# Audio tower: f32 bias rows written by ScalarE, a later read of gamma and beta, and new work lists

## The chip, the cores and the metric

The kernel runs on one core of a Trainium2 chip. The metric is the time of one launch on the device in microseconds. Times are medians of several runs; the profile is one execution of its own.

## What is computed

Sixteen batches of x, 64 channels by 250 steps, go through a depthwise convolution with three taps, a linear map to 128 features and a layer norm; then one attention layer over the 250 tokens of a batch, and a feed-forward layer with lower triangular weights.

```python
def tok(x):                                   # x: (16, 64, 250)
    x_sp = conv3(x, conv_w) + conv_b[None, :, None]          # per channel
    m = einsum('btc,dc->btd', swap(x_sp), lin_w) + lin_b + emb.mean(axis=0)
    return layernorm(m) * ln_g + ln_b                        # over d, 128 wide
def attn(x, kernel):
    WQ, WK, WV = x @ kernel[0], x @ kernel[1], x @ kernel[2]
    QK = einsum('bso,bto->bst', WQ, WK)
    c0 = argmin(sum(QK, axis=2)[0])                          # a row of batch 0
    A = softmax(QK / 8); A[:, c0, :] = 0
    return A @ WV
def ffn(x, W1, b1, W2, b2):
    return gelu(x @ tril(W1).T + b1) @ tril(W2).T + b2
h = tok(x)
h = h + attn(layernorm(h), kernel)
out = h + ffn(layernorm(h), W1, b1, W2, b2)
```

## The kernel before

Two batches are a pair: their 2 x 64 channels fill the 128 partitions, so x is read in eight pairs (k = 0 to 7), and the linear map of both is one product with a block matrix, lin_blk. The 250 tokens of a batch stand on 125 partitions as two tiles (a = 0, 1). All products are f32, but for the bias products below. Everything stays on the chip between input and output.

Each engine has a list of calls at the end of its block, written out by hand (or by a planner) in the order in which it issues; an engine works through its list strictly in order, and semaphores make it wait. So the order of the lists is the schedule.

The steps of a pair k: first_tap (L696, ScalarE; for pairs 0 and 1 own_tap, DVE), second_tap (L988) and third_tap on DVE give the convolution xc. project_bias (L345, TensorE) starts the PSUM bank of the pair with the bias row, the same on all 125 partitions, and project_half (L362) adds the two products of a with start=False. For pair 1 the bias product is f32, mean_w by the centred rows emb_c; for the others it is bf16: DVE splits the row into three bf16 rows (split_hi to row_low, L937 to L961, called from L1095), whose sum with a matrix of ones gives it back. project_first does pair 0 by halves. squares (L687, ScalarE) sums the squares of each token; POOL makes the inverse root (head_root_x, and from pair 3 on shared_root for two norms together); scale_x (DVE) multiplies by root and gamma, and head_beta (DVE, pairs 0 and 1) or add_beta (POOL) adds beta.

The steps of a batch b in attention: moments_1 and gather_1 (DVE), root (POOL), normalize_1 (ScalarE), turn_n1 (TensorE, a transpose), out_n1t (ScalarE), queries and values (TensorE), out_pv (ScalarE; out_p0 and out_v0 for batch 0), scores (TensorE), row_max (DVE), exps (ScalarE), turn_a (TensorE), out_at (ScalarE), attend (TensorE), residual (DVE). Batch 0 also gives the row to be left out: row_sums (TensorE), then find_best and find_place on DVE, on which turn_a(0) waits.

The feed-forward layer goes by turns of a pair (four tiles): moments_2, gather_2 (DVE), second_root (POOL), normalize_2 (DVE), turn_n2 (TensorE), out_n2t (ScalarE), up (TensorE), gelu (ScalarE), down (TensorE), finish (DVE). add_b2 (POOL) has added b2 to the residual before. The last pair has one turn of four tiles, whose down and finish (L1072) are done in two parts of two tiles (down_last, L509).

PSUM has eight banks, all in use: bank_x0 and bank_x1 are shared by taps and projections of the pairs in turn (x_bank, L46), bank_o serves pair 3 and then all attend products, bank_s0 and bank_s1 the scores and later the results y.

SyncE issues the reads of x, the weights and nearly all writes of the output; ScalarE's queue issues the read of tok_w and, second, of rows_sb (gamma, beta and b2, each copied to 125 partitions).

Of the kernel before, what the change touches and what calls it, by code (L numbers as in the profile page):

```python
# [5 lines left out]
ALU = mybir.AluOpType  # L6
# [10 lines left out]
def audio_tower(nc, x, tok_pack, weights, rows, out):  # L17
# [12 lines left out]
    with ExitStack() as ctx:  # L30
# [19 lines left out]
        def x_tile(k, n):  # L50

            b, a = n // 2, n % 2
            if k == 0:
# [15 lines left out]
        y_ps = [t[0:H, :].rearrange("p (n d) -> p n d", d=D) for t in bank_s]  # L69
        y_last = [bank_s[1][0:H, 0:2 * D].rearrange("p (n d) -> p n d", d=D),  # L70
                  bank_at[0:H, 0:2 * D].rearrange("p (n d) -> p n d", d=D)]
# [11 lines left out]
        mean_w = sb("mean_w", [128, H])  # L83
        cb_rest = sb("cb_rest", [C + 1, D])
        cb_hi = sb("cb_hi", [C + 1, D], BF16)
        cb_mid = sb("cb_mid", [C + 1, D], BF16)
        cb_rows = sb("cb_rows", [C + 1, D], BF16)
        ones_b = sb("ones_b", [C + 1, H], BF16)
# [10 lines left out]
        rows_sb = sb("rows_sb", [H, 3 * D])  # L99
        gamma = rows_sb[:, 0:D]  # L100
        beta_4, b2_4 = (rows_sb[:, n * D:(n + 1) * D].unsqueeze(1).broadcast_to((H, 4, D)) for n in (1, 2))
# [60 lines left out]

        def p_sb(b):
            return pv_sb[b % 4][:, 0:T]

        def v_sb(b, a):
# [10 lines left out]
        tri_ready, warm_ready, mean_w_ready, ones_ready, rows_zeroed, means_ready, emb_centred, lin_ready = (  # L177
            sem(n) for n in ("tri_ready", "warm_ready", "mean_w_ready", "ones_ready", "rows_zeroed", "means_ready",
                             "emb_centred", "lin_ready"))
        cb_mm, cb_hi_ready, cb_rest_ready, cb_mid_ready, cb_ready, qk_mm, qk_step, qk_ready, wv_mm, wv_ready, w1_mm, w1_ready = (  # L180
            sem(n) for n in ("cb_mm", "cb_hi_ready", "cb_rest_ready", "cb_mid_ready", "cb_ready", "qk_mm", "qk_step", "qk_ready",
# [23 lines left out]
        def _(sp):  # L205
# [14 lines left out]
            for b in (0, 1):  # L220
                sp.wait_ge(y_ready, NP + b)
                sp.dma_start(out_pairs[NP - 1][0:WIDE, b], hb_rows[0:WIDE, NP - 1, b]).then_inc(out_done, 16)
            sp.wait_ge(out_done, 16 * (2 * NP + 1))

        @block.gpsimd
        def _(pool):
# [33 lines left out]
            def second_root(turn, first, count):  # L260

                cols = slice(4 * first, 4 * (first + count))
                pool.wait_ge(stats2, 2 * (first + count))
                pool.tensor_tensor(ve_2[:, cols], mv_2[:, cols, 1], eps[:, 0:4 * count], ALU.add).then_inc(ve2_ready, 1)
                pool.wait_ge(ve2_ready, turn)
                pool.tensor_tensor(root_2[:, cols], ve_2[:, cols], neg_half[:, 0:4 * count], ALU.pow)\  # L266
                    .then_inc(root2_ready, 1)
# [6 lines left out]
            def add_b2(k):  # L274
                pool.wait_ge(resid_ready, 2 * k + 2)
                pool.tensor_tensor(hb_all[:, k, :, :], h_tiles[:, k, :, :], b2_4, ALU.add).then_inc(hb_ready, 1)  # L276
# [38 lines left out]
            shared_root(2)  # L315
            mask(0)
            mask(1)
            add_b2(0)
            add_beta(5)
            shared_root(3)  # L320
            add_b2(1)
            add_beta(6)
            shared_root(4)
            add_beta(7)
            shared_root(5)
            second_root(1, 0, 2)
            add_b2(2)
            second_root(2, 2, 2)
            add_b2(3)
            add_b2(4)  # L330
            add_b2(5)
            second_root(3, 4, 2)
            second_root(4, 6, 1)
            second_root(5, 7, 1)
            add_b2(6)
            add_b2(7)
        @block.tensor
        def _(pe):
            def keep_warm(count):

                for _ in range(count):
                    nc.tensor.matmul(bank_pv[:, :], warm_l[:, :], warm_r[:, :].unsqueeze(1).broadcast_to((128, 8, 64)),
                                     start=True, stop=True)

            def project_bias(k):  # L345

                dst = x_bank(k)[0:H, :].rearrange("p (a d) -> p a d", d=D)
                before = (0, 0, 1, 0, 4, 6, 10, 12)[k]
                if before:
                    pe.wait_ge(x_scaled, before)  # L350
                if k == 1:
                    nc.tensor.matmul(dst, mean_w[:, :], emb_c[:, :].unsqueeze(1).broadcast_to((128, 4, D)),
                                     start=True, stop=True)
                else:
                    pe.wait_ge(ones_ready, 1)
                    pe.wait_ge(cb_ready, 3)
                    if k >= 4:
# [920 lines left out]
```

## Time and profile before

| | us |
|---|---|
| median of three runs | 94.83 |
| the three runs | 94.83, 94.59, 95.0 |
| the profiled execution | 94.69 |
| its span, first to last instruction | 92.9 |

The granted clock of TensorE is 1.0 in the whole span, the higher of its two levels, 2.4 GHz. The span is what the engines' records cover; the time of an execution is that and 1.8 us around it. DVE is VectorE, ACT ScalarE, POOL GpSimd, SP SyncE; PEld is TensorE's weight load, which runs beside its products. L12 is line 12 of the kernel. Ends of products are modelled, so a busy TensorE is not one at its peak.

### The profile page before, as it was taken

The numbers are of one execution on the slowest core, as the hardware profiler recorded it, in microseconds if no ns is written. First come the engines' busy times: TensorE is split into PE (matmuls) and PEld (weight loads), VectorE is DVE, ScalarE is ACT, GpSimd is POOL, SyncE is SP. The second block draws the span as 40 slices with busy tenths as digits, with TensorE's granted clock in tenths as the row PEclk, the third lists the DMA queues.
The fourth block names the chain that finished last, engine by engine and source line by source line (L and its number), as shares of the span: only waits on it lengthen the run. The fifth ranks groups of instructions, "written<-read, shape, count | busy, mean of one in ns | idle before, by whom it ended". The sixth has DMA issues, their size and how long they took to land.

```text
span 92.9 us, 2013 instructions
## 1 busy us (share of the span) xinstructions
PE 87.2 (94%) x567; PEld 73.9 (80%) x567; DVE 74.4 (80%) x296; ACT 69.3 (75%) x215; POOL 47.8 (51%) x70
## 2 busy tenths in 40 slices
PE   4999699999999999999999999999999999999940
PEld 1356567789999999999999999999997877787840
DVE  3279997999698998869998895988989688793560
ACT  1666799899999969977889976697758983565200
POOL 7006398676554386539525519703996305791000
PEclk9999999999999999999999999999999999999999
DMA  2896000000000000000000000000000003036565
GB/s 17 213 280 212 0 0 4 4 0 0 7 0 0 0 0 0 7 4 0 0 4 4 0 7 0 0 0 0 0 0 7 0 0 110 0 110 169 162 175 167
DMA packets 3973, 3.86 MB, mean 42 GB/s; under 512 B 429, under 2 KB 3962, under 8 KB 3962
## 3 DMA queue, kind: packets, MB, share of 16 engines
q1 hardware_dynamic: 3610, 3.35, 12.8%
q10 hardware_dynamic: 352, 0.38, 1.5%
q8 instruction: 5, 0.08, 0.4%
q14 instruction: 6, 0.05, 0.2%
HBM read 1.68 MB, written 2.05 MB: 40 GB/s over the span
## 4 chain that ended last, share of the span: by engine, by line
PE 80%; DVE 9%; DMA 5%; issue 1%; SPq 0%; DVEq 0%
PE bank_o L483 15%; PE bank_s L458 15%; PE bank_at L470 8%; PE bank_pv L434 7%; PE bank_pv L443 7%; PE bank_s L518 7%; DMA x_all<-x_dram 5%; PE bank_x L366 4%; PE bank_x L496 4%; PE bank_nt L507 4%; PE bank_pv L507 4%; PE bank_nt L423 4%; DVE hb_all L1078 2%; DVE tap_a L994 1%; DVE xc L1000 1%; PE bank_o L366 1%
## 5 line engine op out<-in xcount | busy, mean ns | idle before, releaser
L483 PE MATMUL bank_o<-pv,at_sb 125*125 125x129 f32 x128 | 16.8, 273 | 0.0
L458 PE MATMUL bank_s<-n1t,pv 128*125 128x250 f32 x64 | 16.1, 374 | 0.0
L483 PEld LDWEIGHTS bank_o<-pv,at_sb 125*125 125x125 f32 x128 | 15.6, 187 | 0.1
L772 ACT ACTIVATE a<-bank_s,neg_max 125x250 f32<-125x250 f32 x32 | 13.4, 482 | 1.0 <-DVE neg_max L1039 1.0
L1039 DVE TENSOR_REDUCE neg_max<-bank_s 125x2 f32<-125x500 f32 x16 | 10.7, 668 | 2.2 <-PE bank_s L458 2.1
L458 PEld LDWEIGHTS bank_s<-n1t,pv 128*125 128x125 f32 x64 | 11.0, 187 | 0.9
L780 ACT ACTIVATE at_sb<-bank_at 125x500 f32<-125x500 f32 x16 | 9.6, 597 | 2.4 <-PE bank_at L470 1.8
L276 POOL TENSOR_TENSOR hb_all<-h_all,rows_sb 125x512 f32<-125x512 f32 x8 | 10.9, 1384 | 0.0
L765 ACT ACTIVATE pv<-bank_pv 128x508 f32<-128x508 f32 x15 | 9.0, 602 | 2.1 <-PE bank_pv L443 2.0
L272 POOL TENSOR_TENSOR h_all<-h_all,rows_sb 125x512 f32<-125x512 f32 x6 | 7.6, 1271 | 5.7 <-DVE h_all L1013 5.7
L1050 DVE SCALAR_TENSOR_TENSOR h_all<-bank_o,rinv_keep,h_all 125x128 f32<-125x128 f32 x32 | 9.8, 346 | 0.6
L470 PE MATMUL bank_at<-ident,a 125*125 125x125 f32 x64 | 9.6, 273 | 0.0
L434 PE MATMUL bank_pv<-n1t,qk_w 128*128 128x250 f32 x32 | 9.5, 378 | 0.0
L257 POOL TENSOR_TENSOR root_all<-ve_all,neg_half 125x8 f32<-125x8 f32 (+1 forms) x6 | 9.2, 1541 | 0.5
L518 PEld LDWEIGHTS bank_s<-w_sb,g_sb 128*125 128x125 f32 x60 | 7.4, 187 | 2.1 <-issue 2.1
L443 PE MATMUL bank_pv<-wv_c,n1t 128*125 128x128 f32 x60 | 9.0, 272 | 0.0
L443 PEld LDWEIGHTS bank_pv<-wv_c,n1t 128*125 128x125 f32 x60 | 8.5, 187 | 0.5
L747 ACT ACTIVATE n<-h_all,root_all 125x128 f32<-125x128 f32 x24 | 8.3, 409 | 0.7 <-POOL root_all L257 0.7
L470 PEld LDWEIGHTS bank_at<-ident,a 125*125 125x125 f32 x64 | 8.5, 188 | 0.1
L1068 DVE TENSOR_TENSOR n<-h_all,root 125x512 f32<-125x512 f32 x8 | 7.2, 896 | 1.3 <-POOL root L266 1.3
L692 ACT ACTIVATE squared<-bank_x 125x128 f32<-125x128 f32 x26 | 7.2, 294 | 1.3 <-PE bank_x L412 0.8
L518 PE MATMUL bank_s<-w_sb,g_sb 128*125 128x128 f32 x60 | 7.8, 274 | 0.1
(137 smaller groups left out, 183.7 us busy)
## 6 DMA issues: line engine op xcount, KB each, us to landing
out_dram<-hb_all SPq DMA_DIRECT2D x7, 224.0 KB
x_all<-x_dram SPq DMA_DIRECT2D x8, 125.0 KB, 4.9
out_dram<-hb_all SPq DMA_DIRECT2D x2, 112.0 KB
w_sb<-weights_dram SPq DMA_DIRECT2D x1, 192.0 KB, 5.6
rows_sb<-rows_dram ACTq DMA_DIRECT2D x1, 187.5 KB
out_dram<-hb_all SPq DMA_DIRECT2D x6, 26.0 KB
tok_w<-tok_dram ACTq DMA_DIRECT2D x1, 130.0 KB, 3.1
w_sb<-weights_dram SPq DMA_DIRECT2D x1, 128.5 KB, 5.2
```

The lines of the kernel that those rows point to most:

```text
L257: pool.tensor_tensor(root_all[:, i, lo:8], ve_all[:, i, lo:8], neg_half[:, lo:8], ALU.pow)\
L276: pool.tensor_tensor(hb_all[:, k, :, :], h_tiles[:, k, :, :], b2_4, ALU.add).then_inc(hb_ready, 1)
L434: last = nc.tensor.matmul(p_ps, qk_w[:, :], n1t[b % 2][:, :], start=True, stop=True)
L443: last = nc.tensor.matmul(dst[:, a, 0:D], n1t[b % 2][:, a * H:(a + 1) * H], wv_c[:, :], start=True, stop=True)
L458: last = nc.tensor.matmul(s_ps[b % 2][:, a, :], p_sb(b)[:, a * H:(a + 1) * H], n1t[b % 2][:, :], start=True, stop=True)
L470: last = nc.tensor.transpose(at_ps[:, c, a * H:(a + 1) * H], a_sb[b % 2][:, a, c * H:(c + 1) * H], ident[0:H, 0:H])
L483: last = nc.tensor.matmul(o_ps[:, a, 0:DV], at_sb[:, c, a * H:(a + 1) * H], v_sb(b, c), start=(c == 0), stop=(c == 1))
L518: last = nc.tensor.matmul(dst[:, n, :], g_sb[:, j, col:col + H], w2_t, start=True, stop=True)
L772: last = nc.scalar.activation(a_sb[b % 2][:, a, :], s_ps[b % 2][:, a, :], ACT.Exp, bias=neg_max[b % 2][:, a:a + 1])
L780: nc.scalar.activation(at_sb[:, :, :], at_ps, ACT.Copy).then_inc(at_ready, 1)
L1039: nc.vector.tensor_reduce(neg_max[b % 2][:, :], s_ps[b % 2], AX_X, ALU.max, negate=True)\
L1050: last = nc.vector.scalar_tensor_tensor(h_all[:, b, a, :], o_ps[:, a, 0:D], rinv_keep[:, a:a + 1], h_all[:, b, a, :], ALU.mult, ALU.add)
```

## The change

- ScalarE copies the bias row, an f32 sum over the same product as before but on all 125 partitions, once to SBUF (out_cb) and then writes it four times side by side into the bank of pairs 1 and 3 to 7 (write_bias). project_half waits for that and adds to it. Only pair 2 keeps a bias product, now f32. The bf16 split on DVE, its six instructions and two fills, is gone.
- The first tap of pair 1 moves from DVE to ScalarE; ScalarE does the taps of pairs 1 and 2 ahead of squares(0).
- gamma and beta are read by SyncE behind x of pair 3, b2 alone behind pair 7; ScalarE's queue only reads tok_w.
- The last pair goes through the feed-forward layer in two turns of one batch each (turn gives pair, first tile, count and the batches needed; there are nine turns). The very last results are added tile by tile, into banks at and o, and written by five transfers instead of three.
- The warming products write three banks in turn.
- All four lists are in a new order. In the first half first_tap(4) stands ahead of out_p0, turn_a(0) ahead of the products of pair 5, and squares and normalize_1 come later beside exps; the beginnings of two lists are in the diff.

```diff
-        mean_w = sb("mean_w", [128, H])
+        mean_w = sb("mean_w", [128, 128])
+        cb_sb = sb("cb_sb", [H, D])
...
+        def turn(j):
+            return (j, 0, 4, 2 * j + 2) if j < NP - 1 else (NP - 1, 2 * (j - NP + 1), 2, j + NP)
...
         @block.sync
-            for k in range(2, 5):
+            for k in range(2, 4):
                 sp.dma_start(x_all[:, k, 1:T + 1], x_pairs[k]).then_inc(landed_x[k], 16)
+            sp.dma_start(rows_sb[:, :], rows[:, 0:2 * D].broadcast_to((H, 2 * D))).then_inc(landed_rows, 16)
+            sp.dma_start(x_all[:, 4, 1:T + 1], x_pairs[4]).then_inc(landed_x[4], 16)
             sp.dma_start(w_sb[:, 3 * D:5 * D + 1], weights[:, 3 * D:5 * D + 1]).then_inc(landed_f, 16)
             for k in range(5, NP):
                 sp.dma_start(x_all[:, k, 1:T + 1], x_pairs[k]).then_inc(landed_x[k], 16)
+            sp.dma_start(b2_sb[:, :], rows[:, 2 * D:3 * D].broadcast_to((H, D))).then_inc(landed_b2, 16)
...
         @block.tensor
             def project_bias(k):
-                dst = x_bank(k)[0:H, :].rearrange("p (a d) -> p a d", d=D)
-                before = (0, 0, 1, 0, 4, 6, 10, 12)[k]
...
-                    nc.tensor.matmul(dst, ones_b[:, :], cb_rows[:, :].unsqueeze(1).broadcast_to((C + 1, 4, D)),
-                                     start=True, stop=True)
+                pe.wait_ge(x_scaled, 1)
+                nc.tensor.matmul(x_bank(k)[0:H, :].rearrange("p (a d) -> p a d", d=D), mean_w[:, 0:H],
+                                 emb_c[:, :].unsqueeze(1).broadcast_to((128, 4, D)), start=True, stop=True)
             def project_half(k, a):
                 pe.wait_ge(conv_ready, k + 1)
+                if k != 2:
+                    pe.wait_ge(bias_ready, max(k - 1, 1))
...
             project_first(0)
             bias_row()
+            qk_product()
             project_first(1)
-            project_bias(1)
-            qk_product()
             project_half(1, 0)
             wv_centre()
-            project_bias(2)
             project_half(1, 1)
             qk_centre(0)
-            qk_centre(1)
+            project_bias(2)
             project_half(2, 0)
             project_half(2, 1)
+            qk_centre(1)
             turn_n1(0)
-            project_bias(3)
             project_half(3, 0)
+            queries(0)
             project_half(3, 1)
-            queries(0)
...
         @block.scalar
-            act.dma_start(rows_sb[:, :], rows.broadcast_to((H, 3 * D))).then_inc(landed_rows, 16)
...
+            def out_cb():
+                act.wait_ge(cb_mm, 1)
+                nc.scalar.activation(cb_sb[:, :], bank_s[0][0:H, 0:D], ACT.Copy).then_inc(cb_out, 1)
+            def write_bias(k):
+                act.wait_ge(cb_out, 1)
+                if k >= 4:
+                    act.wait_ge(conv_ready, k + 1)
+                nc.scalar.activation(x_bank(k)[0:H, :].rearrange("p (a d) -> p a d", d=D),
+                                     cb_sb[:, :].unsqueeze(1).broadcast_to((H, 4, D)), ACT.Copy).then_inc(bias_ready, 1)
...
+            first_tap(1)
+            first_tap(2)
             squares(0)
+            out_cb()
+            write_bias(1)
+            write_bias(3)
             squares(1)
-            first_tap(2)
+            out_wv()
             out_qk(0)
-            first_tap(3)
             squares(2)
             out_qk(1)
+            first_tap(3)
             squares(3)
+            normalize_1(0)
             out_qk(2)
-            normalize_1(0)
-            out_wv()
             squares(4)
+            out_n1t(0)
             squares(5)
-            out_n1t(0)
+            spread_rows()
             normalize_1(1)
-            spread_rows()
+            first_tap(4)
             out_p0()
...
         @block.vector
             own_tap(0)
             second_tap(0)
             third_tap(0)
-            own_tap(1)
             second_tap(1)
+            second_tap(2)
             third_tap(1)
-            split_hi()
-            split_rest()
-            split_mid()
-            row_hi()
-            row_low()
+            third_tap(2)
             scale_x(0)
-            row_mid()
             head_beta(0)
-            second_tap(2)
             moments_1(0)
             gather_1(0)
             scale_x(1)
-            third_tap(2)
             head_beta(1)
...
-            finish(7, 0)
-            finish(7, 1)
+            finish(7)
+            finish(8)
+            finish(9)
```

## Rows read from the trace of the kernel before

**Rows 1.** The page: busy time and share of each engine.
```profile
PE 87.2 (94%) x567; PEld 73.9 (80%) x567; DVE 74.4 (80%) x296; ACT 69.3 (75%) x215; POOL 47.8 (51%) x70
```

**Rows 2.** Windows: stretch, length, busy us of each engine, clock, DMA share, GB/s.
```profile
18.00:24.00 6.00, 5.94 (x35) 5.30 (x34) 5.57 (x24) 6.00 (x23) 4.07 (x6) 1.00 0.01 3
24.00:30.00 6.00, 6.00 (x47) 5.68 (x47) 5.06 (x23) 5.97 (x23) 3.23 (x4) 1.00 0.00 0
30.00:36.00 6.00, 6.00 (x47) 5.65 (x46) 5.67 (x24) 5.25 (x15) 4.09 (x6) 1.00 0.00 0
36.00:44.00 8.00, 8.00 (x53) 7.38 (x52) 6.62 (x27) 6.92 (x25) 4.62 (x5) 1.00 0.01 3
```

**Rows 3.** Chain of waits: start, length in us, what; from 13.50 to 88.26 TensorE.
```profile
13.50 1.14 PE bank_o L366 x4
...
15.92 0.84 PE bank_s L458 x4
...
22.70 0.44 PE bank_at L470 x4
...
86.50 1.76 PE bank_s L518 x16
...
89.53 0.42 DVE hb_all L1078
```

**Rows 4.** The same chain: bias products of pairs 4 and 6.
```profile
18.21 0.40 PE bank_x L359
...
34.14 0.22 PE bank_x L359
```

**Rows 5.** Timeline of the head: start, length, engine, line, what.
```profile
6.41 0.28 ACT L692 ACTIVATE squared<-bank_x 125x128 f32<-125x128 f32 x1 [0.80 <-PE bank_x L412]
...
7.15 0.28 DVE L940 CAST cb_hi<-bank_s 65x128 bf16<-65x128 f32 x1
...
7.51 0.71 POOL L235 TENSOR_TENSOR root_head<-ve_head,neg_half 125x2 f32<-125x2 f32 x1
...
8.45 0.61 DVE L1013 SCALAR_TENSOR_TENSOR h_all<-bank_x,root_head,rows_sb 125x128 f32<-125x128 f32 x2
...
12.05 0.68 ACT L747 ACTIVATE n<-h_all,root_head 125x128 f32<-125x128 f32 x2
```

**Rows 6.** Timeline of ScalarE behind it: two of four squares, out_p0, the tap.
```profile
12.90 0.28 ACT L692 ACTIVATE squared<-bank_x 125x128 f32<-125x128 f32 x1
...
13.42 0.28 ACT L692 ACTIVATE squared<-bank_x 125x128 f32<-125x128 f32 x1
...
15.19 0.37 ACT L726 ACTIVATE pv<-bank_pv 128x250 f32<-128x250 f32 x1
...
15.46 0.56 ACT L703 ACTIVATE bank_x<-x_all,tok_w 128x250 f32<-128x250 f32 x1
...
15.95 0.26 ACT L692 ACTIVATE squared<-bank_o 125x128 f32<-125x128 f32 x1
```

**Rows 7.** Windows of the loads; landing of x of pairs 2 to 4.
```profile
4.00:4.50 0.50, 0.50 (x2) 0.15 (x1) 0.47 (x2) 0.50 (x4) 0.00 (x0) 1.00 0.56 98
...
6.50:7.00 0.50, 0.50 (x4) 0.26 (x2) 0.47 (x2) 0.49 (x4) 0.00 (x0) 1.00 1.09 370
...
DMA to landing us min/median/max: 5.3/5.4/5.5
```

**Rows 8.** Groups: the copy into at_sb (busy, mean ns); timeline: find_place.
```profile
L780 ACT ACTIVATE at_sb<-bank_at 125x500 f32<-125x500 f32 x16 | 9.6, 597 | 2.4 <-PE bank_at L470 1.8
...
21.61 0.42 DVE L971 FIND_INDEX8 best_at<-best,bank_at 125x8 uint32<-125x250 f32 x1
```

**Rows 9.** Timeline of the end; what SyncE waits for last (us, times, longest).
```profile
81.15 1.75 DVE L1068 TENSOR_TENSOR n<-h_all,root 125x512 f32<-125x512 f32 x1 [0.58 <-POOL root L266]
...
88.82 0.60 PE L518 MATMUL bank_at<-w_sb,g_sb 128*125 128x128 f32 x4
...
SPq L30 <- DMA out_dram<-hb_all: 2.1, 1, 2.1
```

More of the change, by code:

```diff
@@ L272, in add_beta, with add_b2 @@
                 pool.tensor_tensor(h_tiles[:, k, :, :], h_tiles[:, k, :, :], beta_4, ALU.add).then_inc(h_ready, 1)
-            def add_b2(k):
-                pool.wait_ge(resid_ready, 2 * k + 2)
-                pool.tensor_tensor(hb_all[:, k, :, :], h_tiles[:, k, :, :], b2_4, ALU.add).then_inc(hb_ready, 1)
+            def add_b2(j):
+                k, first, count, batches = turn(j)
+                tiles = slice(first, first + count)
+                pool.wait_ge(landed_b2, 16)
+                pool.wait_ge(resid_ready, batches)
+                pool.tensor_tensor(hb_all[:, k, tiles, :], h_tiles[:, k, tiles, :], b2_4[:, 0:count, :], ALU.add).then_inc(hb_ready, 1)
             def mask(n):
@@ L494, in turn_n2 @@
                     pe.wait_ge(n2t_ready, j - 1)
-                for n in range(4):
-                    last = nc.tensor.transpose(t2_ps[j % 2][:, n * H:(n + 1) * H], n2[:, j, n, :], ident[0:H, 0:H])
+                k, first, count, _ = turn(j)
+                for n in range(count):
+                    last = nc.tensor.transpose(t2_ps[j % 2][:, n * H:(n + 1) * H], n2[:, k, first + n, :], ident[0:H, 0:H])
                 last.then_inc(t2_mm, 1)
@@ L579, in _ @@
             scores(4)
+            queries(5)
+            project_half(5, 1)
+            values(5)
+            turn_a(3)
             turn_n1(6)
-            queries(5)
-            values(5)
             attend(2)
-            turn_a(3)
+            scores(5)
             queries(6)
-            scores(5)
-            project_bias(6)
             values(6)
@@ L827, in _ @@
+            out_n1t(2)
+            exps(0)
             first_tap(5)
-            out_n1t(2)
+            normalize_1(3)
+            out_pv(2)
+            out_at(0)
+            out_n1t(3)
+            exps(1)
+            normalize_1(4)
+            out_pv(3)
+            normalize_1(5)
+            write_bias(5)
+            out_n1t(4)
             squares(8)
-            normalize_1(3)
-            exps(0)
-            out_pv(2)
             squares(9)
-            out_n1t(3)
-            normalize_1(4)
@@ L850, in _ @@
             first_tap(6)
-            out_n1t(6)
-            out_pv(5)
-            normalize_1(7)
+            out_at(3)
             exps(4)
-            out_at(3)
+            out_pv(6)
+            out_n1t(7)
+            write_bias(6)
             normalize_1(8)
-            out_n1t(7)
-            out_pv(6)
+            first_tap(7)
+            exps(5)
+            out_pv(7)
+            out_at(4)
             normalize_1(9)
-            exps(5)
-            out_at(4)
-            first_tap(7)
+            out_n1t(8)
@@ L1150, in _ @@
             moments_1(8)
-            second_tap(6)
             moments_1(9)
+            moments_2(1)
             gather_1(8)
             gather_1(9)
+            residual(2)
+            second_tap(6)
+            row_max(5)
             third_tap(6)
-            moments_2(0)
-            residual(2)
-            row_max(5)
             scale_x(10)
-            moments_2(1)
+            scale_x(11)
             residual(3)
-            scale_x(11)
+            moments_2(2)
+            second_tap(7)
+            moments_2(3)
+            moments_1(10)
+            third_tap(7)
             row_max(6)
-            second_tap(7)
-            third_tap(7)
-            moments_1(10)
             moments_1(11)
@@ L1202, in _ @@
             residual(9)
[L1203 removed]
             moments_2(8)
[L1205 to L1210 removed]
+            moments_2(9)
             gather_2(6)
             gather_2(7)
[L1213 removed]
+            row_max(12)
+            normalize_2(1)
+            residual(10)
+            row_max(13)
+            normalize_2(2)
+            residual(11)
+            row_max(14)
```

440 lines of the change are left out of this document (201 added, 239 removed).

## Prediction

> **What bounds the kernel now.** I read the page first: TensorE is busy for 87.2 of 92.9 us, DVE for 74.4, ScalarE for 69.3 [rows 1]. A share of the whole says little here, so the second view is the windows by stage: from 18 to 44 us TensorE is busy nearly all the time, and ScalarE too from 18 to 30 (6.00 and 5.97 of 6.00), with 0.75 free in 30 to 36 and 1.08 in 36 to 44 [rows 2]. So two engines are full at once through the first half. The third view, the chain of waits, shows three parts: a head in which DVE sets the pace, an unbroken stretch of TensorE from 13.50 until 88.26, and a tail to the end of the last DVE addition at 89.95 [rows 3]. In the tail TensorE still does the last batches' products; its last record ends at 89.42 [rows 9]. The fourth view is the timeline of the head, where I look for what starts when [rows 5, 6].
>
> **Part 1, bias products off TensorE.** Within the unbroken stretch the bf16 bias products of pairs 4 to 7 go: 0.40 for the first and 0.22 for each of three more [rows 4], 1.06 us, all on the path as long as TensorE stays full. Pairs 1, 2 and 3 lie ahead of 13.50, where TensorE has free time; the f32 product of pair 1 goes as that of pair 2 becomes f32: nothing. The wider bias row (125 instead of 65 weight columns) streams the same 128 columns: nothing.
>
> **Part 2, the same work on ScalarE.** Each write_bias is a copy of 125x512 elements; the nearest row is the 125x500 copy into at_sb with 597 ns [rows 8], and as neighbours overlap by a tenth (a tap of 0.56 is followed 0.49 later, rows 6) it holds the queue some 0.48. There are six: pairs 1 and 3 in the head, 4 and 5 before 30 us, 6 and 7 after; 2.9 us. Beside them stand the copy out_cb (0.25) and first_tap(1), 0.49 from start to start like the tap of pair 4 [rows 6]. In the head ScalarE's sum from 5.6, when lin_blk is done, to normalize_1(0) is: the taps of pairs 1, 2 and 3 1.5, squares(0) to (3) 2.1 (0.52 each, from 12.90 to 13.42, rows 6), out_cb 0.25, two bias writes 1.0, three small copies 0.6, and short waits of 0.3, estimated: 5.75, which is 11.35. Before, normalize_1(0) began at 12.05 [rows 5], since ScalarE stood idle in between. That idle time is the cover; if x of pair 2 comes late, it is gone, because first_tap(2) now stands ahead of squares(0), and the root, scale_x(0) and everything behind them wait with it.
>
> **Part 3, the head on DVE.** The split goes: five small instructions fill 7.15 to 8.45, where scale_x(0) begins, though its root was ready at 8.22 (7.51 and 0.71) [rows 5]; a sixth follows. Out of the way go also the tap of pair 1 (to ScalarE) and both taps of pair 2 (ahead of scale_x(0), while DVE waits for the root). squares(0) began at 6.41, which is 1.81 before that root was done [rows 5]; now two taps stand ahead of it, it begins at about 6.55, and scale_x(0) at about 8.35: only 0.1 earlier. The gain lies behind: from scale_x(0) at 8.45 to 13.50, where TensorE takes the result of third_tap(3), are 5.05 us; less the sixth copy and two taps (0.2 and twice 0.4) that is 4.05, so 12.4 if nothing waits. I take 12.65, since second_tap(3) now waits for a later first_tap(3). The stretch of TensorE starts 0.85 earlier; the bounds are 0 and 1.1.
>
> **Part 4, the loads.** x of pairs 2 to 4 landed 5.3 to 5.5 us after its issue [rows 7]; so pair 2, issued at 2.2, was there at 7.6. With that time first_tap(2) would hold squares(0) until 8.1. But while gamma, beta and b2 were being read on ScalarE's queue, the engines moved 98 GB/s in 4.0 to 4.5, against 370 GB/s in 6.5 to 7.0 [rows 7]. The new kernel issues this read behind pair 3, so x0, x1 and the weights no longer share with it. Its 187.5 KB at the quicker rate are 0.5 us, at the slower rate 2.0: pair 2 lands between 5.6 and 7.1. I take 6.0, nearest to the slow rate, which is the one that stood at the time. The Trainium skill, DMA: Bandwidth & Descriptors, section on why a DMA increments its semaphore by 16 and not by 1, says that a copy runs on the largest number of engines up to 16 that divides its outermost count, which for 125 copies of a row is 5; by this the old read blocked 5 engines for long, pair 2 would land nearer 5.6 now, and the new read would itself be slow. No view here shows single engines; the low rate agrees. Gamma is needed at 8.35. It is issued at about 3.1, where pair 4 was; with that one's 5.5 it lands at 8.6, and less the 0.5 to 2.0 of above between 6.6 and 8.1, so I let nothing wait for it. x4, the FFN weights and x5 to x7 are pushed back by its issue, about 0.6 us; x4 is first read at 15.46 [rows 6], which covers it. b2 goes last and is used only behind the first residual.
>
> **Part 5, new waits in the stretch.** Every project_half but those of pairs 0 and 2 now waits for ScalarE, and behind it on TensorE's queue stand the next batches' transposes and scores. I walked the new lists by hand with the steps of the old trace. scores(0) needs out_p0, which now stands behind first_tap(4): out_p0 began 3.14 behind normalize_1(0) (15.19 and 12.05), and now 3.14+0.49-0.09 (out_qk(2) in the place of out_wv), at 14.9; it ends at 15.3 and scores(0) starts there instead of at 15.92 [rows 3, 5, 6]: 0.6 gained of 0.85, a wait of 0.25. turn_a(0) stood at 22.70 [rows 3] and had both halves of pair 5 in front; find_place ended at 22.03 [rows 8]. By the new order TensorE is there at 20.25, and DVE, which has moments 3 to 5 ahead of find_place, at 20.75: 0.5. attend(1) waits for residual(0), behind row_max(2), two moments and two gathers: 0.25. Sum 1.0 us; the bounds are 0 (the order fits) and 2.0 (each again as much). ScalarE has no room in 18 to 30, but squares(10), (11) and normalize_1(6) move out of it (1.6 us) as two bias writes and a tap come in (1.5).
>
> **Part 6, the end.** The last addition is over 128 columns instead of 256. The old one lasts 0.42 [rows 3]; at an estimated 0.3 this gives back 0.1. The last transfer is half as large, but the wait of 2.1 us behind it [rows 9] I leave unchanged. One more turn stands before the last products: residual(15), moments, gather, root, normalize_2(8). TensorE has the products of three and a half turns between attend(15) and turn_n2(8), some 7 us, and the chain needs about 6.4. But normalize_2(6) may meet POOL's add_b2, as the one at 81.15 did, which took 1.75 [rows 9]. I add 0.1; bounds 0 and 0.7.
>
> **The sum.** -1.06 -0.85 +1.0 -0.1 +0.1 = -0.9, made against the profiled execution: 94.69 (span 92.9 and 1.8 around it), which is 0.14 under the median of the three runs. 94.69-0.9 = 93.8; I say 93.75.
>
> **The rivals.**
> 1. The lists fit, and no new wait arises: -1.06 -0.85 -0.1 = -2.0, 92.7. For it: the old order left TensorE no idle time in 24 to 44 us. Against it: ScalarE is nearly as full.
> 2. ScalarE becomes the bound from 12 to 44 us; this is the slower end. Four bias writes put 1.9 us there, where it had some 2.1 us free in all, of which TensorE's shorter list takes 1.06 away: 0.9 sticks out. If x of pair 2 lands at 7.6 too, the gain of the head is lost, the waits of part 5 come on top, and the saved products only turn into idle time of TensorE: 94.69+0.9 = 95.6 at the worst. It decides from the point where exps(3) ends later than in the old kernel.
> 3. Gamma and beta land at 8.8 or later: scale_x(0) waits 0.5 to 0.8, and all behind it: 94.4. For it: four x transfers stand before it, and by the skill's rule above it runs on few engines. Against it: 187.5 KB less in front.
> 4. The end stalls: normalize_2(6) and (8) late by 0.6 in sum: 94.3.
> 5. The moved load does nothing, pair 2 lands as before, and ScalarE holds: the gain of part 3 is lost, 94.6.
>
> **How the numbers follow.** Forecast 0.45 (own range 93.1 to 94.3), rival 1 0.18, rivals 3 and 4 0.18 together, rival 5 0.07, rival 2 0.12. The range reaches from 92.5 (rival 1) to 94.9, and leaves out rival 2. A measurement tells 0.5% (0.47 us) from no change; against the median 94.83 faster means under 94.36. Forecast, rival 1 and two thirds of 3 and 4 give 0.75, rival 5 and the rest 0.12, rival 2 0.13.
>
> **What would show it.** In the new profile: TensorE's idle time between 13 and 36 us near 1.0; squares(0) at about 6.5 and no ScalarE wait for x_all above 0.3; scale_x(0) at 8.35 with no wait for rows_sb; third_tap(3) ending near 12.65; normalize_1(0) near 11.35; ScalarE full until about 40; the last DVE addition ending near 89.0. The prediction is wrong if ScalarE waits long for x of pair 2, or TensorE waits above 2 us in sum for ScalarE.

## The result, and the profile after

The kernel after took 95.59 us (median of 21 executions, 94.73 to 96.59), the kernel before beside it 94.90 (21 executions): ratio 1.0055, 95% interval 1.0035 to 1.0075. In a second measurement, made for a second profile, it took 95.22 (94.77 to 95.86, ratio 1.0036, 1.0007 to 1.0066). The forecast was 93.75 us, with a range from 92.5 to 94.9: it is slower by about half a percent instead of faster by one.

The profiled execution of the first measurement was a disturbed one, so the lines below are from an execution of the same kernel in the second: 95.35 us, span 93.6, 1.8 around it (before: 94.69, 92.9, 1.8). What an execution takes around its span is known to 0.05 us, since spans are given to 0.1.

The page's busy times:

```profile
PE 86.6 (93%) x563; PEld 73.2 (78%) x563; DVE 72.0 (77%) x289; ACT 73.9 (79%) x225; POOL 48.3 (52%) x73
```

The windows from 18 to 44 us (columns as in [rows 2]):

```profile
18.00:24.00 6.00, 6.00 (x41) 5.40 (x40) 5.48 (x24) 5.96 (x20) 4.16 (x6) 1.00 0.01 3
24.00:30.00 6.00, 6.00 (x42) 5.66 (x41) 4.64 (x22) 6.00 (x23) 2.65 (x4) 1.00 0.00 0
30.00:36.00 6.00, 6.00 (x45) 5.72 (x44) 5.90 (x26) 6.00 (x23) 2.84 (x4) 1.00 0.00 0
36.00:44.00 8.00, 8.00 (x58) 7.33 (x57) 7.56 (x39) 7.90 (x28) 3.38 (x5) 1.00 0.01 3
```

Against [rows 1, 2], TensorE has 0.6 us less work in all and ScalarE 4.6 more; from 18 to 44 us ScalarE is busy for 25.86 of 26.00, before for 24.14. The timeline of the head, with squares(0), the two bias rows, root, scale_x(0) and the first of the products of project_half(3, 0):

```profile
6.51 0.25 ACT L685 ACTIVATE squared<-bank_x 125x128 f32<-125x128 f32 x1
...
7.30 0.60 ACT L709 ACTIVATE bank_x<-cb_sb 125x512 f32<-125x512 f32 x1
7.63 0.83 POOL L239 TENSOR_TENSOR root_head<-ve_head,neg_half 125x2 f32<-125x2 f32 x1
7.84 0.58 ACT L709 ACTIVATE bank_o<-cb_sb 125x512 f32<-125x512 f32 x1
...
8.57 0.61 DVE L1006 SCALAR_TENSOR_TENSOR h_all<-bank_x,root_head,rows_sb 125x128 f32<-125x128 f32 x2 [0.67 <-POOL root_head L239]
...
12.88 0.31 PEld L366 LDWEIGHTS bank_o<-lin_blk,xc 128*125 128x125 f32 x2 [0.41 <-DVE xc L993]
```

Before, this last step stood at 13.50 [rows 3]; now it stands at 12.88, so the head gives 0.62. The timeline of the end:

```profile
88.35 0.42 DVE L1073 TENSOR_TENSOR hb_all<-bank_s,hb_all 125x256 f32<-125x256 f32 x1 [1.21 <-PE bank_s L522]
...
88.59 0.38 PE L522 MATMUL bank_o<-w_sb,g_sb 128*125 128x128 f32 x2
...
88.86 0.29 DVE L1073 TENSOR_TENSOR hb_all<-bank_at,hb_all 125x128 f32<-125x128 f32 x1
...
89.43 0.29 DVE L1073 TENSOR_TENSOR hb_all<-bank_o,hb_all 125x128 f32<-125x128 f32 x1 [0.28 <-issue]
89.75 0.33 SPq L226 DMA_DIRECT2D out_dram<-hb_all  x1
89.76 0.35 ACTq L953 DMA_DIRECT2D out_dram<-hb_all  x1
```

SyncE's last wait (us, times, longest):

```profile
SPq L30 <- DMA out_dram<-hb_all: 3.1, 1, 3.1
```

TensorE's last record ends at 88.97, 0.45 earlier than the 89.42 of before [rows 9]. The last addition ends at 89.72 and before at 89.95 [rows 3]: 0.22 of the gain are gone, and in front of that addition DVE stands idle for 0.28 us with nothing to wait for ("issue"). Then the last wait is 3.1 us, before 2.1 [rows 9]; it is 3.1 in the profile of the first measurement too, so it belongs to the kernel and not to one execution. From the end of the last addition to the end of the span it is 3.8 us, before 2.9. So three differences, -0.45, +0.22 and +0.9, give the +0.7 of the span. The loss arises behind TensorE's last product, in 4.6 us in which hardly anything is computed.

### The profile page after: what moved, and what is told of

Its sections match the earlier page's. It is cut to its first block, busy times and chain, and to the rows that moved or that the text cites. A ratio compares the mean times of both kernels' runs of the same rounds, so it can differ in the third digit from the quotient of the medians.

```text
span 94.3 us, 2031 instructions
## 1 busy us (share of the span) xinstructions
PE 87.7 (93%) x563; PEld 73.7 (78%) x563; DVE 72.1 (76%) x289; ACT 74.1 (79%) x225; POOL 47.9 (51%) x73
## 4 chain that ended last, share of the span: by engine, by line
PE 90%; ACT 3%; issue 1%; DVE 1%; DVEq 0%
PE bank_o L486 15%; PE bank_s L461 15%; PE bank_at L473 8%; PE bank_s L522 7%; PE bank_pv L446 7%; PE bank_pv L437 7%; PE bank_x L366 5%; PE bank_nt L512 4%; PE bank_x L500 4%; PE bank_nt L426 4%; PE bank_pv L512 3%; PE bank_o L351 2%; PE bank_pv L351 1%; PE bank_x L351 1%; PE bank_x L415 1%
## 5 line engine op out<-in xcount | busy, mean ns | idle before, releaser
L777 ACT ACTIVATE a<-bank_s,neg_max 125x250 f32<-125x250 f32 x32 | 13.5, 486 | 0.0
L283 POOL TENSOR_TENSOR hb_all<-h_all,b_sb 125x512 f32<-125x512 f32 (+1 forms) x9 | 10.7, 1201 | 0.0
L1021 DVE BATCH_NORM_STATS2 bn<-h_all 125x6 f32<-125x128 f32 x32 | 7.4, 280 | 1.3 <-POOL h_all L276 1.2
L270 POOL TENSOR_TENSOR root<-ve,neg_half 125x8 f32<-125x8 f32 (+2 forms) x6 | 7.8, 1305 | 0.5
```

The lines of the kernel that those rows point to most:

```text
L283: pool.tensor_tensor(hb_all[:, k, tiles, :], h_tiles[:, k, tiles, :], b2_4[:, 0:count, :], ALU.add).then_inc(hb_ready, 1)
L777: last = nc.scalar.activation(a_sb[b % 2][:, a, :], s_ps[b % 2][:, a, :], ACT.Exp, bias=neg_max[b % 2][:, a:a + 1])
```

## The experiments

All were timed in 5 rounds against the kernel before on the same chip; "after" is the kernel after.

**1. Eight turns.** The last pair in one turn and in three last transfers, as in before, on the head and the middle of after:

```diff
...
-                return (j, 0, 4, 2 * j + 2) if j < NP - 1 else (NP - 1, 2 * (j - NP + 1), 2, j + NP)
+                return (j, 0, 4, 2 * j + 2)
...
```

> The changed kernel with the last pair in one feed-forward turn again, as in the kernel before (products, additions and three transfers as there; the order of the last lists written anew for it). If the end is what ate the gain (theory B: TensorE waits of 0.3 before the last transposes, 0.3 before the last up product and 0.3 before the last down products, a late last addition of 0.3, and a last wait that is 1.0 longer), this is 1.0 to 1.8 us faster than the changed kernel and 0.5 to 1.3 faster than the one before. If the head and the stretch ate it (theory A, with the waits of the forecast), this is within 0.3 us of the changed kernel.

Measured: 95.54, ratio 1.0067 (1.0045 to 1.0090). The last wait is back at 2.0, but TensorE waits 1.5 us for the last normalize_2: my order was poor, and the run tells nothing on that theory. It shows something else: span 92.9, as before, and still 95.44 us for this execution. 2.5 us lie around the span, not 1.8.

**2. Three last transfers**, with after's nine turns:

```diff
...
-            sp.dma_start(out_pairs[NP - 1][0:WIDE, 1, 0:D], hb_rows[0:WIDE, NP - 1, 1, 0:D]).then_inc(out_done, 16)
-            sp.dma_start(out_pairs[NP - 1][WIDE:H, 1], hb_rows[WIDE:H, NP - 1, 1]).then_inc(out_done, 16)
+            sp.dma_start(out_pairs[NP - 1][0:WIDE, 1], hb_rows[0:WIDE, NP - 1, 1]).then_inc(out_done, 16)
...
-            act.dma_start(out_pairs[NP - 1][0:WIDE, 1, D:2 * D], hb_rows[0:WIDE, NP - 1, 1, D:2 * D]).then_inc(out_done, 16)
+            act.dma_start(out_pairs[NP - 1][WIDE:H], hb_rows[WIDE:H, NP - 1]).then_inc(out_done, 16)
...
```

> The changed kernel with its two last turns kept, but the last pair written by three transfers as before (112 rows of each batch by SyncE, the 13 last rows of both by ScalarE's queue), both of the last ones behind the last addition. It tells the transfers apart from the turns. If the five transfers (half rows of 512 bytes, two issues in a row on ScalarE's queue) make the last wait longer, it falls from 3.1 to about 2.1 us here and the time by 0.5 to 1.0. If the turns alone cost, the time stays within 0.2.

Measured: 94.93, ratio 0.9996 (0.9972 to 1.0020); last wait 2.2 us, as expected; the median is 0.3 us under after's, less than the 0.5 to 1.0 expected. I took this for proof that five transfers cost time by themselves. Run 14 corrects that.

**3. Warm-up products into one bank:**

> The changed kernel with seven of the nine warming products in one bank, as before, and only the first two in the other banks. If writing three banks in turn is why TensorE's clock rose late, it rises at about 5 us here and the time falls by 0.5 to 0.7 us. If it has nothing to do with it, the time stays within 0.2 of the changed kernel.

Measured: 95.22, ratio 1.0048 (1.0020 to 1.0076), no gain. The record of the higher granted clock starts at 5.21 us here, and in the two profiled executions of after, which write three banks, at 4.35 and 7.19: the banks do not decide it. In this execution rival 3 is to be seen on DVE, in a kernel that loads just as after does:

```profile
9.16 0.61 DVE L1006 SCALAR_TENSOR_TENSOR h_all<-bank_x,root_head,rows_sb 125x128 f32<-125x128 f32 x2 [1.27 <-DMA rows_sb<-rows_dram]
```

scale_x(0) waits for gamma until 9.16; in after it starts at 8.57: 0.6 us. Of the profiled executions, this is the only one with that wait.

**4. TensorE's last turns in another order** (turn_n2(8) and down(6) behind up(7)):

> One change to the kernel after: behind down(5) TensorE does up(7), turn_n2(8), down(6), up(8) and no longer down(6), turn_n2(8), up(7), up(8). In the look at the kernel after, TensorE waited 0.7 us for gelu's g_sb at the last turns, 0.4 for n2t and 0.3 for n. Theory A (the split turn costs TensorE idle time because its order is poor): 0.3 to 0.45 us of the 0.7 go, the last addition ends at 89.3 instead of 89.7, ratio 0.996 against the kernel after. Theory B (ScalarE and DVE are simply late with nine turns): the wait only moves to another line, and the time is the same within 0.1 us.

Measured: 95.71, ratio 1.0060 (1.0026 to 1.0094). From project_half(3, 0) to TensorE's last record 76.18 us, against 76.09 in after: theory B for this stretch, the waits only move. The median is 0.5 us above after's, which neither theory had; the intervals of the two ratios overlap.

**5. The last 13 rows of both batches in one transfer:**

> One change to the kernel after: the last 13 rows of both batches go in one transfer behind the last addition; the early transfer of batch 14's 13 rows and the late one of batch 15's are gone, so four transfers are left in place of five. The two transfers of 112 rows with 512 bytes each stay. Theory A (the number of small late transfers, and the 13-row one of batch 15 on the last issue above all, makes the last wait 3.1 us instead of 2.1): the wait behind the last addition falls by about 0.3 to 0.9 us. Theory B (the transfers with 512 bytes in a row make it long): it stays at 2.8 to 3.1 us, and only three transfers with whole rows, as in the run with three, give 2.2.

Measured: 95.00, ratio 1.0006 (0.9981 to 1.0030); last wait 2.4. Four transfers are left. The fall of 0.7 us from 3.1 is as theory A has it, but see run 14.

**6. Gamma and beta in 128 partitions:**

```diff
...
-            sp.dma_start(rows_sb[:, :], rows[:, 0:2 * D].broadcast_to((H, 2 * D))).then_inc(landed_rows, 16)
+            sp.dma_start(rows_sb[:, :], rows[:, 0:2 * D].broadcast_to((128, 2 * D))).then_inc(landed_rows, 16)
...
```

> One change to the kernel after: gamma and beta are read into 128 partitions instead of 125, at the same place of the queue. By the Trainium skill, DMA: Bandwidth & Descriptors, section on why a DMA increments its semaphore by 16 and not by 1, 125 copies of a row run on 5 engines and 128 on 16. Theory A (the read lands late because it runs on few engines): it lands over 0.5 us sooner after its issue, scale_x(0) never waits for rows_sb, and x of pairs 4 to 7 land sooner; the time falls by 0 to 0.4 us. Theory B (four x transfers stand ahead of it): it lands as late as in the kernel after, and the time is the same within 0.1 us.

Measured: 95.24, ratio 1.0027 (0.9997 to 1.0056): the same as after. Theory B, for the time.

**7. The load move undone:**

> Undoes the load move alone: gamma and beta are read as the second transfer of ScalarE's queue, as in the kernel before; b2 and all the rest stay as in the kernel after. Prediction's theory: x of pairs 2 and 3 land 5.3 us after their issue instead of 3.5, so first_tap(2), squares(0), scale_x(0) and the first products of the unbroken stretch start 0.8 to 1.5 us later and the time rises by 0.5 to 1.0 us. Rival (the load move does nothing for the time, since the head is held by DVE and the root): the loads land later, but scale_x(0) moves by under 0.2 us and the time is the same within 0.2 us.

Measured: 96.16, ratio 1.0139 (1.0100 to 1.0178), so 0.9 us slower than after. ScalarE waits for x again:

```profile
7.17 0.59 ACT L696 ACTIVATE tap_a<-x_all,tok_w 128x250 f32<-128x250 f32 x1 [0.91 <-DMA x_all<-x_dram]
7.67 0.25 ACT L685 ACTIVATE squared<-bank_x 125x128 f32<-125x128 f32 x1
```

scale_x(0) is at 9.73 and project_half(3, 0) at 14.04, 1.16 later, with the same 76.09 us behind it. The load move carries the gain of the head; the prediction's theory stands and rival 5 falls.

**8. No bias of pairs 4 to 7:**

> The kernel after without the bias of pairs 4 to 7: ScalarE's write_bias(4) to (7) are gone (some 4 times 0.48 us), and project_half of these pairs begins its bank itself; the part left out is the bias of the projections of 16 of the 32 tiles. Rival 2 (ScalarE is the bound between 12 and 44 us): TensorE's waits in this stretch get shorter, its last record ends 0.5 to 1.0 us earlier and the time is 0.5 to 1.0 us under the kernel after. Prediction's theory (the waits of 1.0 us in the stretch are those of single chains through DVE and POOL, and ScalarE's writes are covered): under 0.3 us.

Measured: 94.67, ratio 0.9987 (0.9951 to 1.0022). From project_half(3, 0) to the last record 75.96 us, 0.13 less than in after: ScalarE's four writes are covered, and rival 2 falls although ScalarE has 0.14 us free in 26 in after. Its own sign does not come either: exps(3) ends at 28.97 in after, before at 30.98. The median is 0.55 us under after's, the size that rival 2 had; in the profiled execution the time isn't gained in that stretch, and where the others gain it is not shown.

**9. One last addition over two tiles**, with three transfers (compare run 2, 94.93):

> The kernel after with the three last transfers of the run with three, and the last batch in one addition over two tiles (both in one bank) in place of two additions of one tile each. In the look at the kernel after, finish(8) started at 88.86 and finish(9) at 89.43 and ended at 89.72. Theory A (the two additions of one tile cost a gap): the last addition starts when TensorE's last product is done, near 89.0, lasts 0.42 as before and ends at 89.4 to 89.5, 0.2 to 0.3 us sooner; ratio 0.997 against the run with three transfers. Theory B: the addition of two tiles waits for the last product, and that eats what it gives back: the same within 0.1 us.

Measured: 95.08, ratio 1.0021 (0.9994 to 1.0048): no gain over run 2. Theory B: the addition waits 0.31 us for TensorE's last product.

**10 and 11. Eight turns in a better order, and gamma in 128 partitions besides:**

> The kernel after with the last pair in one turn and three last transfers, as in the first run of that kind, but with an order that keeps the chain of the last turn short: attend(15) ahead of up(3), moments_2(15) and gather_2(15) ahead of normalize_2(6), and add_b2(7) ahead of the last second_root. In that run TensorE waited 1.45 us for the last normalize_2, which started at 83.25 and took 1.75 beside POOL's add_b2(7). Theory A (head and stretch of the kernel after do give their 0.7 to 0.9 us, and its tail loses them): TensorE's last record ends near 88.4, the last addition near 89.0, the last wait is 2.1, and the time is 0.6 to 0.9 us under the kernel before, ratio 0.991 to 0.994. Theory B (the gain is not there at the end, whatever the tail): ratio 0.998 or more.

> The kernel of the run with eight turns in the new order, and gamma and beta read into 128 partitions. Between gamma in 125 partitions and in 128 lay 0.0 us of the median (95.22 and 95.24, in two calls), but the look with 128 had a span 0.5 us shorter. Theory A (the read of 125 copies is late in some executions and then holds scale_x(0)): the median falls by 0.1 to 0.4 us against the run with 125, and its spread gets narrower. Theory B: no difference beyond 0.1 us.

Measured: 95.41, ratio 1.0068 (1.0033 to 1.0103), and 95.81, ratio 1.0097 (1.0063 to 1.0132). In run 10 the order does a part of what it was to do: TensorE's last record ends at 89.01 (run 1: 89.39, expected 88.4), the last wait is 2.0, and the span is 92.5, 0.4 under before. Yet this execution took 94.98 us, 2.5 around the span. Neither theory foresaw a gain inside the span and a loss outside it. Run 11 is 0.4 us above run 10, which neither of its theories has; the intervals overlap.

What lies there is shown by two more views. The DMA queues (packets within the span, MB, share), run 10:

```profile
q8 instruction: 4, 0.07, 0.3%
q14 instruction: 5, 0.04, 0.1%
```

The windows behind the span's end, run 10 (the last column is GB/s):

```profile
93.00:94.00 1.00, 0.00 (x0) 0.00 (x0) 0.00 (x0) 0.00 (x0) 0.00 (x0) 0.50 0.03 8
94.00:95.00 1.00, 0.00 (x0) 0.00 (x0) 0.00 (x0) 0.00 (x0) 0.00 (x0) 0.50 0.06 16
```

Before and after both have 5 and 6 packets, and 0 GB/s in the windows from 93 to 97 us.

So in run 10 each queue fetches its last block of instructions, 8 and 16 KB, only when the kernel has ended.

**12. Paddings on the kernel of run 10**: 16 waits for something long done, which become 8 instructions (the trace of each engine has 8 more), on DVE, on TensorE, on both; they lie in the head, where the engine waits or ends its warm-up.

```diff
+            for _ in range(17):
+                dve.wait_ge(pads_zeroed, 2)
             dve.wait_ge(landed_tok, 16)
-            dve.wait_ge(pads_zeroed, 2)
...
             keep_warm(9)
+            for _ in range(16):
+                pe.wait_ge(warm_ready, 2)
```

> The kernel of the run with eight turns in the new order (span 92.5 us, 95.41 median), with 8 more instructions on DVE that only wait for something long done, in the head while DVE is idle. In that kernel and the two like it the profile's instruction queues have 4 and 5 packets within the span and one each behind its end (windows 93 to 95 us: 8 and 16 GB/s), and 2.5 us lie around the span; in all others 5 and 6 packets, none behind the end, and 1.7 to 1.9 us. Theory A (DVE's program ends just ahead of a block boundary, and the next block is fetched only when the end code is reached): the counts go to 5 and 6 or at least 4 and 6, the time around the span falls to 1.8 and the median to 94.7 or less. Theory B (another engine's program): 2.5 us stay around the span.

> The same as the run before it, with the 8 instructions on TensorE in place of DVE, behind the warm-up products. Theory A (DVE's block): the other queue's late packet may move into the span, but 2.5 us or nearly so stay around it and the median near 95.4. Theory B (TensorE's block is the one that costs): 1.8 us around the span, median 94.7 or less.

> Both paddings. If the late fetches are the cause of the time around the span: 5 and 6 packets within the span, none behind it, 1.8 us around a span of 92.5 and a median of 94.3 to 94.6, ratio 0.993 to 0.996 against the kernel before; that would be the gain of head and stretch that the prediction counted on, less 0.3. If they are not: 95.4 as without padding.

Measured: 95.55, 94.87 and 94.62 (ratios 1.0063, 0.9988, 0.9963; the last 0.9931 to 0.9995), against 95.41. DVE's padding moves the 8 KB packet into the span and does nothing for the time; TensorE's moves the 16 KB one and gives 0.5 us (theory B, though 94.87 is a little over its 94.7). With both no packet is left behind the end, 1.8 us lie around this span of 92.8, and the late fetches are the cause: 16 instructions that do nothing make the kernel 0.8 us faster.

**13. The same two paddings on after:**

> The kernel after with the same two paddings. In the 21 executions of the first measurement 13 had 2.2 to 2.4 us around the span and 8 had 1.8. Theory A (those 13 had a fetch behind the end, as the profiled one had, and the padding takes the boundary away): the median falls by 0.2 to 0.4 us against 95.22 to 95.59, and the profiled execution has 1.8 us around its span. Theory B (a padding has no effect there): the median stays at 95.2 to 95.6.

Measured: 94.32 (93.61 to 95.18), ratio 0.9909 (0.9875 to 0.9943): 0.9 us under after's 95.22, and faster than before. The timeline of its end:

```profile
88.52 0.38 PE L522 MATMUL bank_o<-w_sb,g_sb 128*125 128x128 f32 x2
...
88.79 0.29 DVE L1075 TENSOR_TENSOR hb_all<-bank_at,hb_all 125x128 f32<-125x128 f32 x1
89.01 0.29 DVE L1075 TENSOR_TENSOR hb_all<-bank_o,hb_all 125x128 f32<-125x128 f32 x1
```

Its last wait, and behind it the window behind its end:

```profile
SPq L30 <- DMA out_dram<-hb_all: 1.7, 1, 1.7
```

```profile
93.00:94.00 1.00, 0.00 (x0) 0.00 (x0) 0.00 (x0) 0.00 (x0) 0.00 (x0) 0.50 0.07 16
```

TensorE ends as in after (88.90 and 88.97). But the idle 0.28 ahead of the last addition is gone, and the last wait is 1.7 and not 3.1. So the paddings do help, but by more than theory A had (0.2 to 0.4) and in another place: it had looked for a fetch behind the end, and in after the fetches meet the output inside the span. The 16 KB one now comes at 93.20, behind the end, and 2.0 us lie around the span. The profiled execution is no exception: the median span of the 12 is 92.25, and 93.2 for the kernel before beside them.

**14. One padding, and three transfers with both:**

> The kernel after with the padding on DVE alone. With both paddings its span fell from 93.6 to 92.0 us and its median to 94.32; there the late 8 KB packet of the instruction queues went from 90.3 to 86.6 us and the late 16 KB packet from 90.0 to 93.3, the gap of 0.28 us ahead of the last addition was gone, and the last wait was 1.7 instead of 3.1 us. Theory A (DVE's own fetch makes the gap, the other engine's 16 KB fetch at 90.0 holds up the last output transfers): the gap is gone, the last wait stays at 2.7 to 3.1 us, and the median is 94.9 to 95.2. Theory B (DVE's fetch is the cause of both): last wait 1.7 to 2.2 us, median 94.3 to 94.6.

> The kernel after with both paddings and with three last transfers in place of five. Without paddings three transfers gave 0.3 to 0.6 us (94.93 against 95.22). Theory A (the five transfers were long only because instruction fetches met them): no gain over 94.32, rather 0 to 0.3 us slower, since the last transfer is twice as large; last wait 1.7 to 2.1 us. Theory B (five transfers cost time by themselves): median 94.0 or less.

Measured: 95.23, ratio 1.0029 (1.0000 to 1.0058), with the gap gone (the last addition ends 0.40 behind TensorE's end, 0.75 in after) and a last wait of 2.8; and 94.22, ratio 0.9926 (0.9892 to 0.9959), with a last wait of 1.8. Theory A both times: the 16 KB fetch holds up the output, and three transfers are no better than five once it is away. The gap shows no cost of its own: without it the median is 95.23, with it 95.22, which fits an output that ends with the packets that the fetch holds up.

The packets of the trace give the start of the last block fetches, in us from the span's start, beside the number of last transfers, the last wait and what lies around the span:

```
                       16 KB   8 KB    last transfers  last wait  around
before                 86.22   87.10   3               2.1        1.8
after                  90.06   90.37   5               3.1        1.8
run 1                  94.73   93.96   3               2.0        2.5
run 2                  90.60   90.89   3               2.2        1.9
run 3                  90.65   91.10   5               2.8        1.8
run 4                  90.30   90.56   5               3.0        1.8
run 5                  90.28   90.58   4               2.4        1.7
run 6                  90.03   90.32   5               2.7        1.8
run 7                  91.25   91.55   5               2.5        1.7
run 8                  87.03   91.18   5               2.9        1.8
run 9                  90.72   92.14   3               2.4        1.9
run 10                 94.36   93.57   3               2.0        2.5
run 11                 94.43   93.92   3               1.9        2.6
run 12, DVE            94.40   87.84   3               2.0        2.6
run 12, TensorE        87.18   93.84   3               1.9        1.9
run 12, both           87.35   87.72   3               2.0        1.8
run 13                 93.20   86.54   5               1.7        2.0
run 14, DVE            90.56   87.01   5               2.8        1.8
run 14, 3 transfers    93.76   87.25   3               1.8        1.9
```

With five transfers the last wait is 2.5 to 3.1 where a fetch falls between 90 and 92 us, and 1.7 where none does; with three it is 2.2 and 2.4 with such a fetch and 1.8 to 2.1 without. A 16 KB fetch 1.8 to 1.9 us behind the span's end makes 2.5 to 2.6 around it, one 1.2 us behind 1.9 to 2.0.

The same packets show how the fetch holds up the output. In after the 16 KB packet ends at 91.58. Of the two late transfers of 112 rows, 512 bytes each, seven packets of each start only from 91.56 on, one after the other, until 92.36; seven is a sixteenth of 112, the share of one of the 16 DMA engines. With DVE's padding it is the same seven and seven behind the packet's end at 91.55. With both paddings all output packets are through by 90.92. In run 8, where the 16 KB fetch is early, seven and seven start from 91.49 on, which is the end of the 8 KB packet: so an 8 KB fetch can do it too.

## Why the prediction was wrong

**Part 1** held. **Part 3**: the head was to give 0.85 and gives 0.62. squares(0) came as forecast (6.51 for 6.55), but POOL takes longer: 0.83 for the root, which took 0.71 before [rows 5], and 0.37 for the operation ahead of it, before 0.20. So scale_x(0) starts at 8.57 for 8.35, and the step at 12.88 for 12.65. Where TensorE's granted clock rises later the gain is less: the trace's record of the higher level starts at 4.50 us in before and at 4.35 in after, and ahead of it the warm-up products of 512 columns start 0.43 us apart, so the 1.0 given for the whole span of before holds from there on. It starts only at 6.6 to 7.2 in runs 2 and 9, run 14 with three transfers and the first profile of after. There squares(0) starts at 7.0 to 7.3, and the step stands at 13.3 to 13.5. **Part 2**: the bias writes start 0.54 apart for the 0.48 of the sum, normalize_1(0) at 11.52 for 11.35.

**Part 4** held: x of pairs 2 and 3 lands 3.5 us after its issue and not 5.3 [rows 7], pair 2 near 5.7 for 6.0, and by run 7 the move is worth 1.16 us of the head. Gamma was in time in all profiled executions but one. By the Trainium skill's rule cited there the read runs on few engines; run 6 shows no effect of that on the time.

**Part 5** was right in its sum, and partly by luck. From project_half(3, 0) to TensorE's last record before took 75.92 us (13.50 to 89.42) and after 76.09. The sum had -1.06 +1.0 +0.1 for this stretch, +0.04; measured +0.17. The saved products did turn into waits, and not by ScalarE's lack of time (run 8), but mostly elsewhere than worked out. scores(0) starts at 15.44 for 15.3; find_place ends at 20.13 for 20.75, and turn_a(0), from 20.56, and attend(1) show no wait, where 0.75 us were put. Instead the weight load of turn_n1(1) waits 0.64 (before 0.29), and those of the feed-forward turns wait 1.6 in sum for g_sb, n2t and n, before 0.7. TensorE's idle time between 13 and 36 us, which was to be near 1.0, is 0.24.

**Part 6 is the step that failed**: it left the wait of 2.1 us behind the last transfer unchanged, without asking what else is moved by DMA at that time. The wait is 3.1: +1.0. Of the 1.6 us between the -0.9 of the sum and the +0.7 of the span, the output behind the last addition has 0.9, the last addition 0.3, the head 0.2 and the stretch 0.1. The last addition gives 0.1 back by its size and loses 0.3 in the idle gap, though without the gap the time is the same (run 14). Wait and gap both go with the place of the last instruction blocks: before they are fetched at 86.2 and 87.1, ahead of the last output, after at 90.1 and 90.4, in the middle of it. With both paddings, which change nothing else in the program, the span is 92.0 us, 0.9 under before. That this is the sum on record (-0.9) is in part luck: the last addition ends 0.65 sooner, where the sum had 0.95, and the rest comes from a last wait of 1.7 instead of 2.1, which the prediction did not have. The median of 94.32 is 0.6 above the forecast, with up to 2.3 around the span for 1.8 and a clock that rises later in some executions.

The rivals 1, 2, 4 and 5 fall (for rival 4, the weight loads wait 0.3 for normalize_2 at the end, as before); rival 3 is seen in one execution. None of the five was what happened. Of the signs that the prediction named, the last addition, which was to end near 89.0 and ended at 89.7, pointed to the right place. Of its two signs of being wrong, a long wait for x of pair 2 did not come, and TensorE's waits for ScalarE are not what cost the time (run 8); none of its signs looks behind the last addition.

**Open.** 13 of the 21 executions of the first measurement had 2.2 to 2.4 us around the span; the profiled one of these had one more 8 KB packet, at 96.4 us, behind its end. Why some executions of one kernel have it and others not was not found. Eight instructions shift the 16 KB packet by 3 to 7 us, one way or the other, though of TensorE's 1,126 products and loads eight fill only some 0.6 us; by which rule blocks are laid out was not found either, so a padding must be tried. That the output packets held up are the share of one DMA engine follows from their number and times; no view names the engine. Behind the gap of 0.28 us on DVE its 8 KB packet starts only 0.9 to 1.7 us later, so the gap is no wait for these bytes, and what it is stays open. The kernel before was not run with paddings, so the 0.9% of run 13 is between after with a good place of its blocks and before with the place that it happens to have.

## What to carry to other kernels

When a small change moves the time by under one percent, compare first where TensorE's last record ends and then what follows it: a gain can be there up to that point and be lost behind it. Look at the instruction queues and at the windows around the end, since the fetches moved with the lists and with eight added instructions; a change of this size is to be judged with and without paddings, best on both kernels, or its verdict may be that of the block boundary. The version to keep is after with both paddings: ratio 0.9909, or 0.9926 with three transfers, which are the same within their intervals.

## What the runs showed of the hardware

Instruction blocks come as 16 KB packets for TensorE (its padding moves them) and as 8 KB packets on another queue (DVE's padding moves the last of them); one 16 KB packet takes 0.9 to 1.5 us. Beside the last output this costs 0.8 to 1.4 us of waiting with five transfers, behind the end up to 0.7. The Trainium skill, Runtime: NRT & Kernel Launch, section Instruction fetch mechanics, says that engines refill in blocks of 16 KiB and that this is mostly hidden: the 16 KB packets agree, the 8 KB ones do not, and hidden it is not where it meets the end. DVE shows idle time put down to "issue" shortly before its block is fetched: 0.28 us in all kernels with nine turns and two last additions whose 8 KB fetch comes at 90 us or later, and none in the three where it comes at 87.
